# A causal attention between two mixture-of-experts layers: POOL's scatters and gathers held to the attention's steps, six scatters a step, and the causal mask added by 64-row products

## The chip, the core and the metric

The kernel runs on one core of one Trainium2 chip. TensorE (PE) multiplies matrices into PSUM, ScalarE (ACT) and VectorE (DVE) work on tiles in SBUF and PSUM, GpSimd (POOL) does some elementwise work and issues the indirect DMAs, SyncE (SP) issues most plain DMAs. Each engine runs its own list of instructions in order and waits at semaphores for the others. The metric is the device time in microseconds of one execution, as the median of several runs.

## The reference

Three blocks follow one another on x of 16 x 256 tokens and 128 features (4096 tokens in all), each on a layer norm of x:

```python
x = x + 0.5 * ffn(layernorm(x))          # first FFN
x = x + attention(layernorm(x))
x = x + 0.5 * ffn(layernorm(x))          # second FFN

# attention: 16 heads of 64, causal
logits = (x @ P_q) @ (x @ P_k).T / 8
logits = where(causal, logits, -inf)
y = sum over heads of softmax(logits) @ (x @ P_v) @ P_o.T

# ffn: 64 experts of width 64, 8 per token
scores = sigmoid(x @ gate_w.T)
# of 8 groups of experts the best 4, in these the best 8 experts (with gate_bias)
tw = 2.5 * scores[chosen] / sum(scores[chosen])
y = sum over chosen e of tw[e] * (silu(x @ Wg[e]) * (x @ Wu[e])) @ Wd[e]
y = y + shared expert
```

## The kernel before

**The FFNs.** The tokens are eight chunks of 512. Each FFN computes four chunks densely and four sparsely. Dense: all experts for every token, two experts a slot, 33 slots a chunk: the product with We_gate (L824), with We_up (L828), silu (L868), the gated product (L890), the weight of the expert (L903), the product with We_down (L840). Sparse: each token's normalised row is written once for each of its 8 experts into the DRAM array x_rows, sorted by expert, by indirect DMAs of POOL (`dispatch`, L488; 128 scatters of 128 rows for the 16 tiles of 128 tokens). SP then loads x_rows in quads of 512 rows (`f2q_xq`, L742), TensorE turns them (L582), multiplies with the expert of each tile (L607), turns the hidden values (L616) and multiplies with We_down in 64-row products (L636); SP stores the result into y_rows. 52 quads make one FFN: four of the shared expert, which need no load, and 48 with one. POOL fetches the eight results of each token back with indirect DMAs (`gather`, L524), and VectorE adds them with their weights (L542).

**The order of the second FFN.** Dense chunk 0 (33 slots and 5 to drain), then all quads, then the other three dense chunks, in which the gathers are added. The load of the first quad waits until all 128 scatters have landed (`r.scattered`), as does POOL's `copy_high` (L727), which comes after the scatters on POOL and copies We_down rows for the quads. On SP the first load stands behind the store of the first dense chunk (L2102).

**The attention.** It runs in 64 steps: 16 rows (batches) of 256 tokens, four heads a step. Step k on TensorE: the products for q, k and v of step k (L1193 to L1213; v waits for `oT_done`, VectorE's copy of the step before last), the output product of step k-2 (L1281), four transposes of the probabilities of step k-1 (L1249), the scores of the first pair of heads (`score`, L1228, then the mask L1232), eight transposes (L1249), at one step in four the transposes of the next row and of y, the scores of the second pair, in 26 of the steps a product for the second FFN's routing in the bank of k (`in_k_bank`: L1140, L1148, the count, the ranks L209 and L210, the mix), and the weighing of the values of step k-1 (`weigh_values`, L1264). A score product contracts over 64 channels and uses half of the array's rows, head 0 the lower half, head 1 the upper. The mask is added by a further product into the same bank: an identity of 128 rows (`ident_b`) times a mask of 0 and -1e30 (`mask`), both bf16, 256 columns for one head.

ScalarE in step k: the exponentials of step k-1 (`exp_done` after each pair), the copies of q and k (`k_read`), three copies of the transposed probabilities (`probT_done`, L1386), the copy of v (`v_read`, L1369). VectorE: the copy of oT (L1496), `normalise` of both pairs (L1482, L1487), the additions of gathered rows, the layer norm statistics, the maxima of the first pair (L1504, L1505, then L1508), routing of the second FFN, the maxima of the second pair.

**POOL in the attention.** Its list is written step by step: three gathers of the first FFN's results (up to step 42), the reciprocal root of a layer norm where one is due (L1018 and L1021, L1557 and L1562), and from step 49 (`A_DISPATCH`) one half tile of scatters, 4. Nothing in the list waits for the step itself: POOL runs ahead until it meets a buffer that is in use, a layer norm that VectorE has not prepared, or an index list that is not placed (`idx_done`). The remaining scatters stand at the start of the second FFN. There each is followed by a memset of a spare tile (L143, `space`).

Of the kernel before, what the change touches and what calls it, by code (L numbers as in the profile page):

```python
# [25 lines left out]
H = 16  # L26
# [122 lines left out]
def router(ctx, nc, tag, order, w, x_all, b, x_rows, f):  # L149
# [27 lines left out]
    def on_tensor(pe, misc, take_misc):  # L177
# [21 lines left out]
        def count():  # L199
            last = max(r.n for r in order if r.sparse >= 0)  # L200
            pe.wait_ge(route_step, steps_before(order, last + 1))
            pe.wait_ge(w["padded"], 1)
# [36 lines left out]
    def on_vector(dve, misc):  # L239
# [139 lines left out]
        def plan(i):  # L379
# [12 lines left out]
            elif i == 2:  # L392
                dve.wait_ge(w["padded"], 1)
# [77 lines left out]
    def on_gpsimd(pool):  # L471
# [10 lines left out]
        def dispatch(i, spaced=True):  # L482
            tile, half = divmod(i, 2)
            k, t = divmod(tile, CT)
            if t == 0 and half == 0:
                pool.wait_ge(idx_done, k + 1)
            for j in HALVES[half]:
                nc.gpsimd.indirect_dma_start(  # L488
                    x_rows[:, :], bass.IndirectOffsetOnAxis(ap=b.idx[:, f, CT * k + t, j:j + 1], axis=0),
                    b.xk[:, k, t, :], None).then_inc(scattered, 16)  # L490
                if spaced:
                    b.space(pool)
# [542 lines left out]
GATHER_STEP, ADD_LAG = 3, 4  # L1035


def attention(nc, w, x_all, banks, psum, rows, b, mix_rows, y_rows, first, second, gathered, added):
# [16 lines left out]
    with ExitStack() as ctx:  # L1055
# [61 lines left out]
        def lists_of(k):  # L1117
            return range(max(GATHER_STEP * k, 0), min(max(GATHER_STEP * (k + 1), 0), SPARSE * CT * TOPK))
# [9 lines left out]
        def _(pe):  # L1128
# [87 lines left out]
            def score(c, k, pair):  # L1216
# [333 lines left out]
        def _(pool):  # L1550
# [72 lines left out]
def ffn_first(nc, w, x_all, psum, b, mix_rows, x_rows, y_rows, zero, r, rows, x, dr):  # L1623
# [6 lines left out]
    with ExitStack() as ctx:  # L1630
# [189 lines left out]
        def _(pool):  # L1820
# [21 lines left out]
            nc.gpsimd.memset(w["mask"][:, :], 0.0).then_inc(const_step, 1)  # L1842
            nc.gpsimd.memset(w["ident_b"][:, :], 0.0).then_inc(const_step, 1)
            pool.wait_ge(const_step, 9)
            nc.gpsimd.affine_select(out=w["before"][:, :], in_=w["before"][:, :], compare_op=ALU.is_gt, fill=0.0,
                                    base=0, pattern=[[1, P]], channel_multiplier=-1)
            nc.gpsimd.tensor_copy(w["tile_no"][:, :], w["tile_i"][:, :])
            mask = w["mask"][:, :].rearrange("p (a b) -> p a b", a=2)
            nc.gpsimd.affine_select(out=mask, in_=mask, compare_op=ALU.is_ge, fill=MASKED, base=0,
                                    pattern=[[0, 2], [-1, P]], channel_multiplier=1)  # L1850
            nc.gpsimd.affine_select(out=w["ident_b"][:, :], in_=w["ident_b"][:, :], compare_op=ALU.not_equal,
                                    fill=1.0, base=0, pattern=[[-1, P]], channel_multiplier=1)\
                .then_inc(w["padded"], 1)

            waiting = list(FIRST[1:])
            for i, slot_ in enumerate(SCATTER_AT):
# [4 lines left out]
                dispatch(i)  # L1861
# [79 lines left out]
def ffn_second(nc, w, x_all, psum, b, mix_rows, x_rows, y_rows, r, out, dispatched, gathered, added):  # L1941
# [5 lines left out]
    with ExitStack() as ctx:  # L1947
# [127 lines left out]
        def _(pool):  # L2075
            rstd_of, dispatch = r.on_gpsimd(pool)
            gather = comb.on_gpsimd(pool)
            for i in range(dispatched, 2 * SPARSE * CT):
                if i == dispatched + 3:
                    rstd_of(in_dense[0])  # L2080
                dispatch(i)
# [42 lines left out]
def macaron(nc, x, P_q, P_k, P_v, P_o, gate_w, gate_bias, We_gate, We_up, We_down, Ws_gate, Ws_up, Ws_down, out):  # L2124
# [10 lines left out]
    with ExitStack() as ctx:  # L2135
# [6 lines left out]
        w["ident_b"], w["mask"] = sb("ident_b", [P, P], BF16), sb("mask", [P, 2 * P], BF16)  # L2142
# [22 lines left out]
        ffn_second(nc, w, x_all, psum, b, mix_rows, x_rows, y_rows, second, out_v, tiles // (SEQ // P) * (H // 4) - A_DISPATCH,  # L2165
# [24 lines left out]
```

## Time and profile before

| | us |
|---|---|
| median of 3 runs | 1611.32 (1610.64 to 1612.96) |
| the profiled execution | 1613.64 |
| its span in the profile | 1611.9 |
| TensorE busy | 1528.5 (95%) |
| VectorE busy | 1166.3 (72%) |
| ScalarE busy | 766.3 (48%) |
| POOL busy | 722.5 (45%) |

The stages follow one another: the first FFN up to about 540 us, the attention to about 1109 us, then the second FFN, with its first dense chunk up to 1203 us, the quads up to about 1342 us, and three dense chunks. The granted clock of TensorE, averaged over the span, is 0.984 of 2.4 GHz. How to read it: a busy share says little here, since the engine that is waited for differs from stage to stage. What a stage costs is read from the chain of waits and from the idle time that stands in brackets before an instruction.

### The profile page before, as it was taken

To read this page: it belongs to the slowest core of one execution; us is meant where nothing else is said; L and a number is where in the kernel's file an instruction comes from. 1 tells how busy PE (TensorE), PEld (TensorE's weight loads), DVE (VectorE), ACT (ScalarE), POOL (GpSimd) and SP (SyncE) were. 2 spreads that over 40 slices of the span, in tenths; PEclk is the share of its full clock that TensorE was granted. 3 is DMA by queue.
4 is the path that set the end of the run, shared out by engine and by line. 5 is a ranking of instruction groups with operands and counts; after the bars stand their busy time and mean duration, and the time that the engine had idled before them with its cause. 6 is when DMAs were issued, how large, how long until landed. Compare 5 with 4: busy or idle time off the path is not lost. (4 is left out here: it accounts for less than half of the span.)

```text
span 1611.9 us, 27350 instructions
## 1 busy us (share of the span) xinstructions
PE 1528.5 (95%) x8683; PEld 971.2 (60%) x8683; DVE 1166.3 (72%) x3354; ACT 766.3 (48%) x2105; POOL 722.5 (45%) x1123
## 2 busy tenths in 40 slices
PE   5899999999999899999999998999997999999998
PEld 2344444444788677777777776775446885444443
DVE  4698888765444588989898988765875845768675
ACT  2234223222455577777777776774224552222222
POOL 1000088888222344333334105443883225878730
PEclk9999999999999899999999999999998999999999
DMA  9999655553687111000000001103464884666652
GB/s 184 206 259 249 156 127 140 131 142 93 176 223 206 48 28 28 21 21 21 26 21 24 11 2 38 37 31 92 125 157 135 228 224 112 147 149 146 136 132 65
DMA packets 202043, 181.31 MB, mean 112 GB/s; under 512 B 39408, under 2 KB 154288, under 8 KB 201904
## 3 DMA queue, kind: packets, MB, share of 16 engines
q1 hardware_dynamic: 175056, 132.34, 34.8%
q0 software_dynamic: 16384, 33.59, 7.7%
q10 hardware_dynamic: 10464, 13.63, 2.5%
q8 instruction: 74, 1.21, 0.3%
q14 instruction: 65, 0.53, 0.1%
HBM read 121.83 MB, written 57.67 MB: 111 GB/s over the span
## 5 line engine op out<-in xcount | busy, mean ns | idle before, releaser
L868 ACT ACTIVATE f_hid<-banks 128x512 f32<-128x512 f32 (+1 forms) x264 | 157.6, 597 | 511.6 <-PE banks L828 511.5
L488 POOL DMA_INDIRECT x_rows<-r_xk,r_idx x256 | 264.4, 1033 | 138.6 <-issue 53.3
L890 DVE TENSOR_TENSOR f_hid<-banks,f_hid 128x512 f32<-128x512 f32 (+1 forms) x264 | 181.5, 687 | 145.1 <-ACT f_hid L868 144.9
L840 PE MATMUL banks<-f_hid,wd 128*128 128x512 f32 x528 | 273.3, 601 | 12.5 <-DVE f_hid L903 12.5
L824 PE MATMUL banks<-r_xT_d,gu 128*128 128x512 f32 x528 | 276.4, 605 | 4.7 <-DMA wd<-in_L_ffn_We_down 3.1
L828 PE MATMUL banks<-r_xT_d,gu 128*128 128x512 f32 x528 | 273.5, 600 | 0.0
L903 DVE TENSOR_TENSOR f_hid<-f_mix_wide,f_hid 128x512 f32<-128x512 f32 x256 | 176.0, 687 | 31.9 <-DMA f_mix_wide<-mix_rows 29.5
L840 PEld LDWEIGHTS banks<-f_hid,wd 128*128 128x128 f32 x528 | 99.6, 192 | 146.3 <-issue 120.9
L828 PEld LDWEIGHTS banks<-r_xT_d,gu 128*128 128x128 f32 x528 | 100.8, 191 | 130.1 <-issue 126.5
L824 PEld LDWEIGHTS banks<-r_xT_d,gu 128*128 128x128 f32 x528 | 97.5, 192 | 120.3 <-issue 110.6
L524 POOL DMA_INDIRECT a_g<-y_rows,r_idx x128 | 125.1, 977 | 66.3 <-issue 35.2
L1386 ACT COPY a_probT<-banks 128x512 f32<-128x512 f32 x192 | 106.2, 588 | 101.9 <-PE banks L1249 101.0
L524 POOL DMA_INDIRECT f_g<-y_rows,r_idx x128 | 128.9, 1007 | 41.2 <-issue 20.2
L1487 DVE TENSOR_SCALAR a_prob<-a_prob,a_inv 128x128 f32<-128x128 f32 (+1 forms) x512 | 130.8, 323 | 4.5
L1351 ACT ACTIVATE a_prob<-banks,a_bias 128x256 f32<-128x256 f32 x256 | 127.7, 499 | 0.0
L1228 PE MATMUL banks<-a_kT,a_qT 64*128 64x128 f32 (+1 forms) x1024 | 119.3, 351 | 0.0
L1348 ACT ACTIVATE a_prob<-banks,a_bias 128x128 f32<-128x128 f32 x256 | 99.6, 389 | 30.6 <-DVE a_bias L1508 30.5
L1249 PE MATMUL banks<-ident,a_prob 128*128 128x128 f32 x768 | 106.1, 275 | 2.5 <-ACT a_qT L1361 2.1
L143 POOL MEMSET r_spare<- 128x256 f32 x324 | 106.6, 329 | 0.2
L1264 PE MATMUL banks<-a_probT,a_v 128*64 128x256 f32 (+1 forms) x1024 | 97.3, 332 | 1.5 <-ACT a_probT L1386 0.3
L1249 PEld LDWEIGHTS banks<-ident,a_prob 128*128 128x128 f32 x768 | 89.4, 142 | 12.4 <-issue 3.5
L1504 DVE TENSOR_REDUCE a_top<-banks 128x2 f32<-128x256 f32 x128 | 53.4, 417 | 59.2 <-PE banks L1232 58.4
(243 smaller groups left out, 2879.5 us busy)
## 6 DMA issues: line engine op xcount, KB each, us to landing
f_mix_wide<-mix_rows SPq DMA_DIRECT2D x124, 512.0 KB
x_rows<-zero ACTq DMA_DIRECT2D x12, 1024.0 KB, 5.9
f1q_xq<-x_rows SPq DMA_DIRECT2D x48, 256.0 KB, 3.2
y_rows<-f1q_yq SPq DMA_DIRECT2D x48, 256.0 KB, 2.5
f2q_xq<-x_rows SPq DMA_DIRECT2D x48, 256.0 KB, 3.4
y_rows<-f2q_yq SPq DMA_DIRECT2D x48, 256.0 KB, 2.8
x_rows<-r_xk,r_idx POOLq DMA_INDIRECT x256
wd<-in_L_ffn_We_down SPq DMA_DIRECT2D x7, 512.0 KB, 10.8
```

The costliest lines, as they stand in the source:

```text
L488: nc.gpsimd.indirect_dma_start(x_rows[:, :], bass.IndirectOffsetOnAxis(ap=b.idx[:, f, CT * k + t, j:j + 1], axis=0), b.xk[:, k, t, :], Non ...
L524: nc.gpsimd.indirect_dma_start(g_buf[:, t % GBUFS, j, :], None, y_rows[:, :], bass.IndirectOffsetOnAxis(ap=b.idx[:, f, t, j:j + 1], axis=0 ...
L824: nc.tensor.matmul(gate_bank[g % 3][0:rows, :], w["gu"][:, 0, experts, :].rearrange("p e f -> p (e f)"), x, start=True, stop=True)
L828: nc.tensor.matmul(up_bank[g % 3][0:rows, :], w["gu"][:, 1, experts, :].rearrange("p e f -> p (e f)"), x, start=True, stop=True).then_inc( ...
L840: mm = nc.tensor.matmul(acc[:, :], w["wd"][0:rows, 2 * p, :], d.hid[0:rows, g % HIDS, :], start=(p == 0), stop=(p == PAIRS))
L868: nc.scalar.activation(d.hid[0:rows, g % HIDS, :], gate_bank[g % 3][0:rows, :], ACT.Silu)\
L890: nc.vector.tensor_tensor(d.hid[0:rows, g % HIDS, :], up_bank[g % 3][0:rows, :], d.hid[0:rows, g % HIDS, :], ALU.mult).then_inc(gated, 1)
L903: nc.vector.tensor_tensor(d.hid[:, g % HIDS, :], d.mix_wide[:, n % 2, p % SPREAD, :], d.hid[:, g % HIDS, :], ALU.mult).then_inc(weighted, 1)
L1228: nc.tensor.matmul(scores[pair][h][:, cols], qT[side_rows, i, pair, rows_q], kT[side_rows, i, pair, cols_k], start=(cols.start == 0), stop ...
L1249: mm = nc.tensor.transpose(bank[:, j * P:(j + 1) * P], prob[:, n * P:(n + 1) * P], w["ident"][:, :])
L1351: e = nc.scalar.activation(prob[:, o + P:o + NPB], scores[pair][h][:, P:NPB], ACT.Exp, bias=bias[:, i, pair, 1, h:h + 1], scale=HD ** -0.5 ...
L1487: m = nc.vector.tensor_scalar(prob[:, a:b], prob[:, a:b], inv[:, i, pair, late, h:h + 1], None, ALU.mult)
```

## The change

Three things change.

1. **Scatters.** From step 49 on six scatters are issued in a step of the attention (`SCATTER_STEP`) instead of four. `dispatch` takes a range of single scatters now instead of the number of a half tile. The second FFN starts with those that are left.
2. **POOL's gates.** In each step k POOL's three parts, one gather or two scatters each, wait for a point of that step (`reach`): part 0 for the exponentials of the first pair of step k-1, part 1 for the copy of k, part 2 for the last copy of the transposed probabilities.
3. **The mask.** Identity and mask are stored twice as wide, so that each half of the array's rows holds, in two parts, the 128 rows that it needs: part 0 for query rows 0 to 63, part 1 for 64 to 127. A mask of one head is now two products of 64 rows. For two heads there are four, in the order head 0, head 1 of part 0, head 0, head 1 of part 1. The products have 256 columns as before. POOL builds the two tiles in eight selects on 64 partitions each instead of two on 128, one after another.

```diff
-        def dispatch(i, spaced=True):
-            tile, half = divmod(i, 2)
-            k, t = divmod(tile, CT)
-            if t == 0 and half == 0:
-                pool.wait_ge(idx_done, k + 1)
-            for j in HALVES[half]:
+        def dispatch(lists, spaced=True):
+            for i in lists:
+                tile, j = divmod(i, TOPK)
+                k, t = divmod(tile, CT)
+                if t == 0 and j == 0:
+                    pool.wait_ge(idx_done, k + 1)
                 nc.gpsimd.indirect_dma_start(
                     x_rows[:, :], bass.IndirectOffsetOnAxis(ap=b.idx[:, f, CT * k + t, j:j + 1], axis=0),
                     b.xk[:, k, t, :], None).then_inc(scattered, 16)
...
-GATHER_STEP, ADD_LAG = 3, 4
+GATHER_STEP, SCATTER_STEP, ADD_LAG = 3, 6, 4
...
-                for h in range(2):
-                    diagonal = scores[pair][h][:, :].rearrange("p (a n) -> p a n", a=2)[:, :, 0:P]
-                    mm = nc.tensor.matmul(diagonal, w["ident_b"][:, :], w["mask"][:, :], start=False, stop=True)
+                for part in range(2):
+                    for h in range(2):
+                        side_rows = slice(h * HD, (h + 1) * HD)
+                        diagonal = scores[pair][h][:, :].rearrange("p (a n) -> p a n", a=2)[:, :, 0:P]
+                        mm = nc.tensor.matmul(diagonal, w["ident_b"][side_rows, part, :], w["mask"][side_rows, part, :],
+                                              start=False, stop=(part == 1))
                 mm.then_inc(scores_done, 1)
...
+            def reach(k, part):
+                if k < 1:
+                    return
+                if part == 0:
+                    pool.wait_ge(exp_done, 2 * k - 1)
+                elif part == 1:
+                    pool.wait_ge(k_read, k + 1)
+                else:
+                    pool.wait_ge(probT_done, 3 * k)
+
             for k in range(STEPS):
-                for i in lists_of(k):
-                    gather(i // TOPK, (i % TOPK,), spaced=False)
-                if k >= A_DISPATCH:
-                    dispatch(k - A_DISPATCH, spaced=False)
+                fetched = lists_of(k)
+                for part in range(GATHER_STEP):
+                    reach(k, part)
+                    for i in fetched[part:part + 1]:
+                        gather(i // TOPK, (i % TOPK,), spaced=False)
+                    if k >= A_DISPATCH:
+                        m = SCATTER_STEP * (k - A_DISPATCH) + 2 * part
+                        dispatch(range(m, m + 2), spaced=False)
...
+            for side in range(2):
+                for part in range(2):
+                    mask = w["mask"][side * HD:(side + 1) * HD, part, :].rearrange("p (a b) -> p a b", a=2)
+                    nc.gpsimd.affine_select(out=mask, in_=mask, compare_op=ALU.is_ge, fill=MASKED, base=part * HD,
+                                            pattern=[[0, 2], [-1, P]], channel_multiplier=1).then_inc(const_step, 1)
...
-            for i in range(dispatched, 2 * SPARSE * CT):
-                if i == dispatched + 3:
-                    rstd_of(in_dense[0])
-                dispatch(i)
+            dispatch(range(dispatched, dispatched + 12))
+            rstd_of(in_dense[0])
+            dispatch(range(dispatched + 12, TOPK * SPARSE * CT))
```

On TensorE, in a plain step of the attention, from the transposes L1249 (L1252 after the change) to the weighing of the values. Before:

```order
L1249 MATMUL banks<-ident,a_prob 128x128 x4
L1228 MATMUL banks<-a_kT,a_qT 128x128 x2
L1228 MATMUL banks<-a_kT,a_qT 128x256 x2
L1232 MATMUL banks<-mask,ident_b 128x2x128 x2
L1249 MATMUL banks<-ident,a_prob 128x128 x8
L1228 MATMUL banks<-a_kT,a_qT 128x128 x2
L1228 MATMUL banks<-a_kT,a_qT 128x256 x2
L1232 MATMUL banks<-mask,ident_b 128x2x128 x2
L1264 MATMUL banks<-a_probT,a_v 64x256 x2
```

After:

```order
L1252 MATMUL banks<-ident,a_prob 128x128 x4
L1228 MATMUL banks<-a_kT,a_qT 128x128 x2
L1228 MATMUL banks<-a_kT,a_qT 128x256 x2
L1234 MATMUL banks<-mask,ident_b 128x2x128 x4
L1252 MATMUL banks<-ident,a_prob 128x128 x8
L1228 MATMUL banks<-a_kT,a_qT 128x128 x2
L1228 MATMUL banks<-a_kT,a_qT 128x256 x2
L1234 MATMUL banks<-mask,ident_b 128x2x128 x4
L1267 MATMUL banks<-a_probT,a_v 64x256 x2
```

The mask has four products where it had two, all in the form of the score products; what stands before and behind them is the same.

On POOL, the last gathers and the start of the scatters in the attention, up to the second FFN (L1018 is a layer norm's rstd, L488 the scatter, L1055 and L2074 the ends of blocks). Before:

```order
L1018 TENSOR_TENSOR n_veps<-n_moments,eps 128x2
L1021 TENSOR_TENSOR n_rstd<-n_veps,minus_half 128x2
L488 DMA x_rows<-r_xk,r_idx 24576x128 x12
L1018 TENSOR_TENSOR n_veps<-n_moments,eps 128x2
L1021 TENSOR_TENSOR n_rstd<-n_veps,minus_half 128x2
L488 DMA x_rows<-r_xk,r_idx 24576x128 x16
L1018 TENSOR_TENSOR n_veps<-n_moments,eps 128x2
L1021 TENSOR_TENSOR n_rstd<-n_veps,minus_half 128x2
L488 DMA x_rows<-r_xk,r_idx 24576x128 x32
L1055 UNCONDITIONAL_BRANCH
L2074 UNCONDITIONAL_BRANCH
```

After:

```order
L1018 TENSOR_TENSOR n_veps<-n_moments,eps 128x2
L1021 TENSOR_TENSOR n_rstd<-n_veps,minus_half 128x2
L488 DMA x_rows<-r_xk,r_idx 24576x128 x18
L1018 TENSOR_TENSOR n_veps<-n_moments,eps 128x2
L1021 TENSOR_TENSOR n_rstd<-n_veps,minus_half 128x2
L488 DMA x_rows<-r_xk,r_idx 24576x128 x24
L1018 TENSOR_TENSOR n_veps<-n_moments,eps 128x2
L1021 TENSOR_TENSOR n_rstd<-n_veps,minus_half 128x2
L488 DMA x_rows<-r_xk,r_idx 24576x128 x48
L1055 UNCONDITIONAL_BRANCH
```

The scatters of the attention grow from 60 to 90 at the same places among the others, and the pairs of L488 and L143 that open the second FFN fall from 68 to 38. On the same engine a step's three gathers, with their waits after the change:

```order
L524 DMA a_g<-y_rows,r_idx 128x128 [waits a_exp_done]
L524 DMA a_g<-y_rows,r_idx 128x128 [waits a_k_read]
L524 DMA a_g<-y_rows,r_idx 128x128 [waits a_probT_done]
L1560 TENSOR_TENSOR r_veps<-r_moments,eps 128x2 [waits a_c_ln]
L1565 TENSOR_TENSOR r_rstd<-r_veps,minus_half 128x2 [waits a_c_rstd]
```

The gathers stood there as one row, nine for three steps; the order against the layer norms is unchanged, only the waits are new.

## Rows read from the trace of the kernel before

**Rows 1.** The page: the chain that ended last, shares of the span by line.

```profile
PE banks L824 5%; PE banks L828 5%; PE banks L840 5%; POOL x_rows L488 4%; PE banks L607 3%; PE banks L636 2%; PE banks L582 2%; POOL r_spare L143 1%; PE banks L616 1%; DVE f_hid L890 0%; DVE f_hid L903 0%; DVE x_all L542 0%; DMA f2q_xq<-x_rows 0%; DMA x_rows<-r_xk,r_idx 0%; DVE x_all L909 0%
```

**Rows 2.** The chain in order of time: start us, us, what.

```profile
1213.70 2.28 DMA x_rows<-r_xk,r_idx
1215.99 2.92 DMA f2q_xq<-x_rows
```

**Rows 3.** TensorE's timeline, quads of the second FFN: start us, us, what, [idle before].

```profile
1218.95 1.11 PE L582 MATMUL banks<-ident,f2q_xq 128*128 128x128 f32 x4 [9.44 <-DMA f2q_xq<-x_rows]
...
1226.18 0.66 PE L582 MATMUL banks<-ident,f2q_xq 128*128 128x128 f32 x4
1226.67 1.06 PE L607 MATMUL banks<-gu,f2q_xqT 128*128 x8
...
1229.02 1.06 PE L607 MATMUL banks<-gu,f2q_xqT 128*128 x8
```

**Rows 4.** Windows: busy us of PE, PEld, DVE, ACT, POOL; granted clock, DMA share, GB/s.

```profile
545.00:1105.00 560.00, 541.11 (x4524) 420.03 (x4524) 468.57 (x1665) 418.43 (x1437) 195.85 (x227) 1.00 0.08 23
...
1219.00:1224.00 5.00, 5.00 (x26) 4.45 (x27) 1.02 (x3) 1.34 (x3) 0.53 (x2) 0.50 0.38 108
```

**Rows 5.** Waits over the whole span: us in total, times, longest us.

```profile
DVE a_top L1504 <- PE banks L1232: 58.4, 55, 4.4
...
PE banks L1211 <- DVE a_oT L1496: 16.1, 13, 2.2
```

**Rows 6.** Timelines of POOL and of SP in the second FFN.

```profile
1110.66 0.96 POOL L488 DMA_INDIRECT x_rows<-r_xk,r_idx  x1 [41.13 <-POOLq L1055]
...
1112.11 0.96 POOL L488 DMA_INDIRECT x_rows<-r_xk,r_idx  x1 [0.17 <-issue]
...
1204.26 0.37 SPq L2102 DMA_DIRECT2D out<-x_all  x1
```

**Rows 7.** TensorE's timeline, one attention step, and the last score products alone.

```profile
1058.11 0.38 PE L1193 MATMUL banks<-n_xT_hi,pq_hi 128*128 128x256 f32 x1
...
1061.20 0.60 PE L1249 MATMUL banks<-ident,a_prob 128*128 128x128 f32 x4
1061.73 0.93 PE L1228 MATMUL banks<-a_kT,a_qT 64*128 64x128 f32 x8
1062.59 0.39 PE L1232 MATMUL banks<-mask,ident_b 128*128 128x256 bf16 x2
1062.81 1.04 PE L1249 MATMUL banks<-ident,a_prob 128*128 128x128 f32 x8
1063.78 0.93 PE L1228 MATMUL banks<-a_kT,a_qT 64*128 64x128 f32 x8
...
1065.07 1.52 PE L1264 MATMUL banks<-a_probT,a_v 128*64 128x256 f32 x16
1066.52 0.39 PE L1193 MATMUL banks<-n_xT_hi,pq_hi 128*128 128x256 f32 x1
...
1062.05 0.60 PE L1228 MATMUL banks<-a_kT,a_qT 64*128 64x256 f32 x4
...
1062.28 0.38 PE L1228 MATMUL banks<-a_kT,a_qT 64*128 64x256 f32 x1
```

**Rows 8.** ScalarE's timeline in that step.

```profile
1064.41 0.60 ACT L1369 COPY a_v<-banks 128x512 f32<-128x512 f32 x1
```

**Rows 9.** VectorE's and POOL's timelines in that step; L1508: ns min/median/max.

```profile
1059.10 1.01 DVE L1487 TENSOR_SCALAR a_prob<-a_prob,a_inv 128x128 f32<-128x128 f32 x4
...
1064.07 0.37 DVE L1508 TENSOR_SCALAR a_bias<-a_top 128x4 f32<-128x4 f32 x1
...
1063.51 0.95 POOL L488 DMA_INDIRECT x_rows<-r_xk,r_idx  x1 [0.30 <-issue]
1064.77 0.96 POOL L488 DMA_INDIRECT x_rows<-r_xk,r_idx  x1 [0.30 <-issue]
...
L1508 DVE TENSOR_SCALAR a_bias<-a_top x126: 169/170/405, 546.2 to 1099.9; 128x4 f32<-128x4 f32 x126
```

More of the change, by code:

```diff
@@ L201, in count @@
             pe.wait_ge(route_step, steps_before(order, last + 1))
-            pe.wait_ge(w["padded"], 1)
+            pe.wait_ge(w["padded"], 4)
             take_misc(count_read, 1)
@@ L392, in plan @@
             elif i == 2:
-                dve.wait_ge(w["padded"], 1)
+                dve.wait_ge(w["padded"], 4)
                 ins = V.tensor_copy(scan[:, 0, PAD:], b.cnt_p[:, :])
@@ L1841, in _ @@
             nc.gpsimd.iota(w["tile_i"][:, :], [[P, CT]], base=0, channel_multiplier=CHUNK).then_inc(const_step, 1)
-            nc.gpsimd.memset(w["mask"][:, :], 0.0).then_inc(const_step, 1)
-            nc.gpsimd.memset(w["ident_b"][:, :], 0.0).then_inc(const_step, 1)
+            nc.gpsimd.memset(w["mask"][:, :, :], 0.0).then_inc(const_step, 1)
+            nc.gpsimd.memset(w["ident_b"][:, :, :], 0.0).then_inc(const_step, 1)
             pool.wait_ge(const_step, 9)
             nc.gpsimd.affine_select(out=w["before"][:, :], in_=w["before"][:, :], compare_op=ALU.is_gt, fill=0.0,
-                                    base=0, pattern=[[1, P]], channel_multiplier=-1)
@@ L1847, in _ @@
[L1847 to L1853, printed above, removed]
+                                    base=0, pattern=[[1, P]], channel_multiplier=-1).then_inc(const_step, 1)
@@ new lines, in _ @@
+            nc.gpsimd.tensor_copy(w["tile_no"][:, :], w["tile_i"][:, :]).then_inc(const_step, 1)
+            pool.wait_ge(const_step, 11)
+            done = 11
+            for side in range(2):
[3 more added lines that the diff above has]
+                                            pattern=[[0, 2], [-1, P]], channel_multiplier=1).then_inc(const_step, 1)
+                    pool.wait_ge(const_step, done + 1)
+                    ident = w["ident_b"][side * HD:(side + 1) * HD, part, :]
+                    nc.gpsimd.affine_select(out=ident, in_=ident, compare_op=ALU.not_equal, fill=1.0, base=part * HD,
+                                            pattern=[[-1, P]], channel_multiplier=1)\
+                        .then_inc(w["padded"], 1)
+                    done += 1
+                    pool.wait_ge(w["padded"], 2 * side + part + 1)
@@ L1860, in _ @@
                     pool.wait_ge(zeroed, 16 * len(CLEAR_AT))
-                dispatch(i)
+                dispatch(range(4 * i, 4 * i + 4))
             copy_high = qd.on_gpsimd(pool)
@@ L2077, in _ @@
             gather = comb.on_gpsimd(pool)
-            for i in range(dispatched, 2 * SPARSE * CT):
-                if i == dispatched + 3:
-                    rstd_of(in_dense[0])
-                dispatch(i)
+            dispatch(range(dispatched, dispatched + 12))
+            rstd_of(in_dense[0])
+            dispatch(range(dispatched + 12, TOPK * SPARSE * CT))
             copy_high = qd.on_gpsimd(pool)
@@ L2141, in macaron @@
         w["gw"], w["bias"], w["ident"] = sb("gw", [P, E]), sb("gate_bias", [P, E]), sb("ident", [P, P])
-        w["ident_b"], w["mask"] = sb("ident_b", [P, P], BF16), sb("mask", [P, 2 * P], BF16)
+        w["ident_b"], w["mask"] = sb("ident_b", [P, 2, P], BF16), sb("mask", [P, 2, 2 * P], BF16)
         w["ones"], w["before"] = sb("ones", [P, P], BF16), sb("before", [P, P], BF16)
@@ L2164, in macaron @@
             attention(nc, w, x_all, banks, psum, rows, b, mix_rows, y_rows, first, second, gathered, added)
-        ffn_second(nc, w, x_all, psum, b, mix_rows, x_rows, y_rows, second, out_v, tiles // (SEQ // P) * (H // 4) - A_DISPATCH,
+        ffn_second(nc, w, x_all, psum, b, mix_rows, x_rows, y_rows, second, out_v, SCATTER_STEP * (tiles // (SEQ // P) * (H // 4) - A_DISPATCH),
                    gathered, added)
```

## The prediction

> **What bounds the kernel now.** I read the page first: its busy table and its chain of waits. TensorE is busy for 95% of the span and its lines head the chain, but the chain also holds two of POOL, L488 and L143, with 4% and 1% [rows 1]. L488 is the scatter of token rows into x_rows, L143 the memset that spaces scatters in the second FFN. So there is one place where POOL sets the time.
>
> The chain in order of time finds it [rows 2]: scatters, of which the last is issued at 1213.70 us, 2.28 us until the last one has landed, 2.92 us for the first load of gathered rows (f2q_xq), then TensorE's transposes of L582. TensorE's timeline shows what that costs [rows 3]: L582 starts at 1218.95 after 9.44 us idle, released by that load. The windows show the granted clock: 0.50, so 1.2 GHz, from 1219 to 1224 [rows 4]; in the attention it is 1.00 (2.4 GHz). A quad step is 2.35 us long afterwards (L607 at 1226.67 and at 1229.02), but the first two behind the wait take 7.23 us together (L582 at 1218.95 and, as third, at 1226.18) [rows 3]. The wait therefore costs 9.44 + 7.23 - 4.70 = 12.0 us.
>
> Elsewhere the end is set by TensorE itself. In the attention it is busy 541.11 of 560 us [rows 4], and a plain step is 8.40 us long (first L1193 at 1058.11 and at 1066.52) [rows 7]. The exceptions are 13 steps in which its L1211 (project_v) waits for VectorE's copy of oT, 16.1 us in total and 2.2 at most [rows 5]. There VectorE is behind with the routing of the second FFN. So an instruction more or less on TensorE counts in about 51 of 64 steps.
>
> **Scatter, six a step.** Steps 49 to 63 are 15; at 4 each they issue 60 scatters, at 6 each 90. Left for the second FFN are 38 instead of 68. There a scatter takes 1.46 us with its spacer (1110.66 to 1112.11) [rows 6], so POOL ends 30 x 1.46 = 43.8 us earlier, at about 1170. In the attention one takes 1.26 us (1063.51 to 1064.77) [rows 9]. Six take 7.6 us of an 8.4 us step, and with the row's rstd, in two of the steps, 8.5: POOL just keeps up, and those rstd have two steps until they are used.
>
> What is late once the scatters are not? SP issues the loads behind the store of x_all at 1204.26 [rows 6]. The load then lands at about 1204.26 + 0.37 + 2.92 = 1207.6, up to 1 us later behind the store's own 256 KB. TensorE wants it at 1218.95 - 9.44 = 1209.5. That is hidden, and TensorE has no idle time that would take its clock down. copy_high of POOL starts 44 us earlier too. I take the full -12.0; a load 1 us late would make it about -11.
>
> **The mask by 64-row products.** Before, TensorE goes from 64-row score products to two products on all 128 rows (L1232), then to transposes (L1249). After, four 64-row products stand in two concurrent pairs. Two of L1228's products start together here: four of its entries start between 1062.05 and 1062.28, in two passes 0.22 us apart [rows 7]. A mask product streams 256 columns in bf16, 0.11 us, so two pairs cost 0.22, as the two products do now (1062.59 to 1062.81). The multiplication is not what changes. What changes is where the array changes between forms.
>
> The prices, from starts in [rows 7]. Eight transposes take 0.97 us until L1228 starts, four take 0.53: 0.11 each and 0.09 for going to the 64-row form. The last score pass starts at 1062.28 and the mask at 1062.59, 0.31 instead of 0.22: 0.09 for going back. In the quads L636 is a 64-row product in front of transposes: leaving it costs the same 0.09, and then four transposes L582 take 0.49 (1226.18 to 1226.67) instead of 0.44 [rows 3], another 0.05 while the first weights load uncovered. Behind the bf16 mask that second part is 0.01. So for pair 0 the change moves the switch from a place where it costs 0.10 to one where it costs 0.15: +0.05 us a step. Pair 1 is followed in 26 steps by a product in the k bank (another +0.05 in most), else by weigh_values (L1264). There one switch goes entirely, 0.10. But in a plain step L1264 does not start for that reason: it starts at 1065.07, 0.05 us after a_v is copied (1064.41 + 0.60), and on ScalarE that copy stands behind the two copies of probT which the eight transposes release [rows 7, 8]. The saved 0.10 becomes waiting, and the +0.05 of pair 0 passes through. Only some 5 steps, with a_v early, gain it.
>
> The sum: 51 x 0.05 = 2.6, k bank 22 x 0.05 = 1.1, less 5 x 0.10 = 0.5. scores_done comes up to 0.10 earlier, which shortens the 13 places where VectorE sets the time by 0.05 to 0.10, so less 1.0. Together +2.2 us. Bounds: -2 if entering the transposes costs no more than entering the mask did, +5 if every step pays twice.
>
> The Trainium skill, TensorEngine Tiling (Array Packing), Key Properties, says that changing the tiling mode, not just the tile, drains TensorE. The rows agree that a change costs (0.09 us). Counted by that rule alone a step has five changes instead of six and nothing gets slower, which is my first rival below; the row of L582 says that the changes are not equal in price.
>
> **POOL held to the steps.** Gathers now go out one at each of three points of ScalarE's step instead of nine in a row. They are added four steps later and land in a few us, so VectorE never waits for one; a gather's wait for `added` was met 1 to 2 steps earlier. POOL's rstd come behind the last gather of their step and are used two steps on. What can change is a clash on VectorE. L1508 takes 0.17 us, but 0.37 when it starts at 1064.07, and it ends at 1064.44, with POOL's scatter (1063.51 + 0.95) [rows 9]. Most are not hit: of 126 the median is 170 ns. The first point, exp_done of pair 0, is what releases VectorE's four tensor_scalar of normalise as well, so a hit there becomes regular. In a plain step it is hidden, since the first group of L1487, pair 0's, is done at 1060.11 and the first transposes start at 1061.20 [rows 7, 9]. Where VectorE is behind (13 places, each with some two steps of backlog) up to 0.1 us a step is added, and hits in the old runs of nine go away. I take +0.5, between -1.5 and +3.
>
> The Trainium skill, SBUF — State Buffer, Who interferes with whom, says that a tensor_scalar in a two-port mode and a GpSimd instruction exclude each other completely. The L1508 row agrees, with 0.20 us for one hit; by that rule alone every held issue could hit, and this speaks against the change.
>
> **The rest.** At the start POOL builds mask and ident_b in eight selects with waits instead of two. It ends these at about 10 us and their first use is hundreds of us later: 0. Four more products' instructions on TensorE are hidden in the pairs.
>
> Sum: -12.0 + 2.2 + 0.5 = -9.3 us. The profiled execution took 1613.6 us with a span of 1611.9; the median of the runs is 1611.3. Against it: **1602.0 us**.
>
> **The rivals.**
> 1. The switches are worth the same everywhere, so the attention gains a little: pair 0 -0.01 x 51, five steps -0.10, VectorE's places -1.0, so -2.0, and no clash. -14.0: 1597.3. For it: one change of form less. Against it: L582 behind L636. Chance 0.20.
> 2. The clashes become regular: 13 places x 2 steps x 0.1 x 1 to 2 hits, about +4 instead of +0.5: 1605.5. For it: the shared release. Against it: VectorE is idle 55 times before L1504, 58.4 us in total [rows 5], which absorbs most. Chance 0.13.
> 3. A load or copy_high takes the scatter's place at 1209 and TensorE still idles 2 to 3 us with half the clock behind: gain of 6 to 8 us less 2.7, 1606. Against it: SP has only one store ahead. Chance 0.06.
> 4. The slower side: the 64-row mask products do not run as pairs but one after another, as they write into two banks with a strided pattern that L1228 does not have. Each mask then costs 2 x 0.11 more, 128 x 0.22 = 28 us. Of the 13 waits on VectorE, eight stand alone, one in every four steps, with some 1.1 us each, and absorb 9; the five late ones, 0.4 each, 2. 28 - 11 - 12.0 + 0.5 = +5.5: 1617. It decides from the point where more than half of the second products start 0.1 us after the first. Against it: L1228's pairs start 0.01 apart. Chance 0.06.
> The forecast itself: 0.55.
>
> **How the numbers follow.** Forecast's own range: 1599.5 to 1604.5. With the rivals 1 to 3 the range is 1597 to 1607.5, outside it rival 4 and the tails. About 0.2% (3.2 us) is what a measurement here can tell from no change. Faster: forecast, rivals 1 and 2 and nearly all of 3, 0.90; same 0.04; slower, rival 4 in most of its cases, 0.06.
>
> **What would show it.** Right: L582's wait for f2q_xq is gone, granted clock 1.00 at 1209 to 1215, POOL's last L488 some 44 us earlier; the mask products' starts in pairs 0.01 apart; L1228 to mask 0.22, mask to L1249 0.20, and four or eight transposes 0.05 longer; plain steps 8.45 us instead of 8.40. Wrong: plain steps of 8.40 or less (rival 1), the L1211 waits over 17 us in total (rival 2), L582 still waiting (rival 3), mask products 0.11 apart four times (rival 4).

## The result, and the profile after

The changed kernel takes 1601.53 us (median of 6 runs, 1599.03 to 1604.78), the kernel before 1611.34 beside it; the ratio is 0.9933, with a 95% interval of 0.9913 to 0.9952. Forecast were 1602.0, between 1597.0 and 1607.5. An execution now and then takes several per cent longer at a lower granted clock; one such of e6 (1744.52 us) is left out of its median below.

The span is 1601.1 us instead of 1611.9. Milestones of TensorE's timeline divide both. (The first eight quads make seven entries of L582 in the timeline, since the first entry holds two.)

| stretch | before | after | after - before | forecast |
|---|---|---|---|---|
| attention, first L1193 to the dense run's L824 | 578.60 | 580.66 | +2.06 | +2.7 |
| dense run, to the first quad | 93.28 | 94.80 | +1.52 | 0 |
| start of the first quad to start of the eighth | 25.19 | 13.14 | -12.05 | -12.0 |
| ahead of the attention | 531.46 | 530.31 | -1.15 | 0 |
| all from the eighth quad on | 383.39 | 382.15 | -1.24 | 0 |

**The wait is gone.** TensorE's timeline after, columns as in [rows 3]:

```profile
1205.77 1.04 PE L582 MATMUL banks<-ident,r_xk 128*128 128x128 f32 x8
...
1211.23 0.72 PE L636 MATMUL banks<-wd,f2q_hidT 64*128 64x128 f32 x8
1211.87 0.66 PE L582 MATMUL banks<-ident,f2q_xq 128*128 128x128 f32 x4
...
1214.22 0.66 PE L582 MATMUL banks<-ident,f2q_xq 128*128 128x128 f32 x4
...
1216.56 0.66 PE L582 MATMUL banks<-ident,f2q_xq 128*128 128x128 f32 x4
```

The first L582 on f2q_xq has no bracket: no idle time, where [rows 3] shows 9.44 us. The quads follow at 2.35 us from the first on. The window, and then POOL's timeline, say why:

```profile
1211.00:1216.00 5.00, 5.00 (x49) 4.25 (x47) 3.56 (x9) 2.66 (x7) 0.00 (x0) 1.00 0.29 82
```

```profile
1170.75 1.05 POOL L488 DMA_INDIRECT x_rows<-r_xk,r_idx  x1 [0.17 <-issue]
1171.80 0.33 POOL L143 MEMSET r_spare<- 128x256 f32 x1
1178.35 0.52 POOL L727 COPY f2q_wd_high<-wd 128x128 f32 x2 [6.23 <-DMA x_rows<-r_xk,r_idx]
```

The granted clock is 1.00 where [rows 4] has 0.50, and the last scatter is issued 43 us earlier than in [rows 2]. In the chain's shares POOL no longer stands:

```profile
PE 27%; DVE 3%; ACT 0%; issue 0%
```

**The attention step.** TensorE's timeline, a plain step of after:

```profile
1059.17 0.39 PE L1193 MATMUL banks<-n_xT_hi,pq_hi 128*128 128x256 f32 x1
...
1060.66 0.28 PE L1211 MATMUL banks<-pv_hi,n_xT_hi 128*128 128x256 f32 x1
...
1061.34 1.02 PE L1284 MATMUL banks<-a_oT,po 128*128 128x256 f32 x4
1062.20 0.60 PE L1252 MATMUL banks<-ident,a_prob 128*128 128x128 f32 x4
1062.73 0.93 PE L1228 MATMUL banks<-a_kT,a_qT 64*128 64x128 f32 x8
1063.49 0.39 PE L1234 MATMUL banks<-mask,ident_b 64*128 64x256 bf16 x4
1063.81 1.09 PE L1252 MATMUL banks<-ident,a_prob 128*128 128x128 f32 x8
1064.83 0.93 PE L1228 MATMUL banks<-a_kT,a_qT 64*128 64x128 f32 x8
```

Against [rows 7]: scores to mask 0.76 instead of 0.86, mask to transposes 0.32 instead of 0.22, eight transposes 1.02 instead of 0.97. The sum from L1228 to L1228 is 2.10 instead of 2.05, the +0.05 of the prediction. But the step is still 8.40 long, for its projections are quicker. Here L1193 to L1211 takes 1.49 us and L1211 to L1284 0.68. The same step before, whose [rows 7] are continued here:

```profile
1059.63 0.28 PE L1211 MATMUL banks<-pv_hi,n_xT_hi 128*128 128x256 f32 x1
...
1060.33 1.03 PE L1281 MATMUL banks<-a_oT,po 128*128 128x256 f32 x4
```

takes 1.52 and 0.70: its projections start 0.118 us apart, while after they start 0.114 apart. Of 23 plain steps 19 have the slow spacing before and none after. Steps with a product in the k bank have no such gift (8.46 to 8.55 us, 9.07 to 9.21). The waits on VectorE's copy of oT, after, over the whole span:

```profile
DVE a_top L1507 <- PE banks L1234: 55.5, 54, 4.3
...
PE banks L1211 <- DVE a_oT L1499: 16.1, 13, 2.1
```

Their total of 16.1 us is that of [rows 5].

### The profile page after: what moved, and what is told of

Its sections match the earlier page's. It is cut to its first block and busy times, and to the rows that moved or that the text cites. A ratio compares the mean times of both kernels' runs of the same rounds, so it can differ in the third digit from the quotient of the medians.

```text
span 1601.1 us, 27870 instructions
## 1 busy us (share of the span) xinstructions
PE 1523.2 (95%) x8939; PEld 974.9 (61%) x8939; DVE 1167.1 (73%) x3354; ACT 766.1 (48%) x2105; POOL 717.4 (45%) x1099
## 5 line engine op out<-in xcount | busy, mean ns | idle before, releaser
L488 POOL DMA_INDIRECT x_rows<-r_xk,r_idx x256 | 263.3, 1028 | 125.8 <-issue 51.6
L824 PE MATMUL banks<-r_xT_d,gu 128*128 128x512 f32 x528 | 275.4, 603 | 4.2 <-DMA wd<-in_L_ffn_We_down 2.6
L824 PEld LDWEIGHTS banks<-r_xT_d,gu 128*128 128x128 f32 x528 | 97.3, 192 | 119.5 <-issue 109.9
L1389 ACT COPY a_probT<-banks 128x512 f32<-128x512 f32 x192 | 106.2, 588 | 104.4 <-PE banks L1252 103.5
L1228 PE MATMUL banks<-a_kT,a_qT 64*128 64x128 f32 (+1 forms) x1024 | 119.9, 353 | 0.0
L1252 PE MATMUL banks<-ident,a_prob 128*128 128x128 f32 x768 | 109.7, 279 | 2.5 <-ACT a_qT L1364 2.1
L1252 PEld LDWEIGHTS banks<-ident,a_prob 128*128 128x128 f32 x768 | 86.8, 142 | 24.7 <-issue 16.3
L143 POOL MEMSET r_spare<- 128x256 f32 x294 | 96.7, 329 | 0.2
L1507 DVE TENSOR_REDUCE a_top<-banks 128x2 f32<-128x256 f32 x128 | 53.3, 417 | 55.6 <-PE banks L1234 55.5
```

The costliest lines, as they stand in the source:

```text
L488: nc.gpsimd.indirect_dma_start(x_rows[:, :], bass.IndirectOffsetOnAxis(ap=b.idx[:, f, CT * k + t, j:j + 1], axis=0), b.xk[:, k, t, :], Non ...
L824: nc.tensor.matmul(gate_bank[g % 3][0:rows, :], w["gu"][:, 0, experts, :].rearrange("p e f -> p (e f)"), x, start=True, stop=True)
L1228: nc.tensor.matmul(scores[pair][h][:, cols], qT[side_rows, i, pair, rows_q], kT[side_rows, i, pair, cols_k], start=(cols.start == 0), stop ...
L1252: mm = nc.tensor.transpose(bank[:, j * P:(j + 1) * P], prob[:, n * P:(n + 1) * P], w["ident"][:, :])
```

## The experiments

They ran on four chips, and these fall into two kinds. On two the kernel before takes 1613 to 1614 us (e9 to e11 on one, e12 on another). On the other two it takes 1761 (e1 to e4, and e5 to e8), which nothing in the first two profiles had announced. Each chip ran one batch only, so whether this belongs to the chip or to something else at that hour isn't shown; I speak of chips. So each ratio is to the kernel before on its own chip, and stretches are compared between chips only where the steps repeat to 0.01 us.

| run | what it is | us | ratio to before, 95% | attention | first to eighth quad |
|---|---|---|---|---|---|
| e1 | before + new mask | 1764.48 | 1.0036 [1.0014, 1.0057] | 729.4 | 25.6 |
| e2 | before + gates | 1625.35 | 0.9241 [0.9213, 0.9269] | 593.2 | 27.3 |
| e3 | before + six scatters | 1790.25 | 1.0184 [1.0154, 1.0214] | 766.6 | 13.1 |
| e4 | before + six + gates | 1622.92 | 0.9224 [0.9196, 0.9251] | 603.0 | 13.1 |
| e5 | after | 1630.62 | 0.9257 [0.9230, 0.9285] | 612.4 | 13.1 |
| e6 | before, 1 memset between | 1690.92 | 0.9608 [0.9571, 0.9645] | 655.6 | 27.3 |
| e7 | after, one gate | 1663.44 | 0.9455 [0.9424, 0.9486] | 638.4 | 13.1 |
| e8 | after, mask by head | 1628.04 | 0.9246 [0.9220, 0.9272] | 608.8 | 13.1 |
| e9 | before + five + gates | 1601.22 | 0.9939 [0.9919, 0.9959] | 578.7 | 13.1 |
| e10 | before, 3 memsets between | 1615.24 | 1.0021 [1.0009, 1.0034] | 580.6 | 25.4 |
| e11 | after, 1 memset behind each | 1609.17 | 0.9976 [0.9963, 0.9988] | 587.1 | 13.1 |
| e12 | after, no gates | 1599.52 | 0.9924 [0.9907, 0.9941] | 578.9 | 13.1 |

### e1 to e4: one part at a time

```
e1:  + the four 64-row mask products, mask and ident_b in halves
e2:  + reach(k, part)                     (SCATTER_STEP = 4, old mask)
e3:  + SCATTER_STEP = 6                   (no reach, old mask)
e4:  + SCATTER_STEP = 6, + reach(k, part) (old mask)
```

> The kernel before with the 64-row mask products alone; four scatters a step, POOL not held. Theory (the mask moves a switch of the array's form in front of the transposes): steps with a product in the k bank 0.09 to 0.14 us longer, steps with project_v waiting for VectorE unchanged or shorter, attention +1 to +2 us in the trace, the wait of 9.4 us for f2q_xq stays: 1611 to 1613 us, ratio 1.000 to 1.001. Rival (the longer attention is POOL's doing, the mask is free): attention as before within 0.3 us. Rival (fewer switches pay): attention 1 to 2 us shorter.

> The kernel before with POOL held to the steps alone; four scatters a step, mask by 128-row products. Theory (holding makes hits on VectorE's tensor_scalar regular): VectorE's tensor_scalar grow by about 3 us in total over the attention, the 13 waits of project_v by up to 0.05 us each, attention +0 to +1 us, time 1611 to 1613. Rival (holding spreads the gathers and relieves VectorE): attention up to 1 us shorter, 1610.

> The kernel before with six scatters a step alone; POOL not held, mask by 128-row products. Theory: the whole gain comes from here: the wait for f2q_xq and the clock that falls behind it go, -12.0 us against before, attention within 0.3 us: 1599 to 1600 us, 1.5 to 3 us faster than the changed kernel. Rival (without the gates 30 more scatters crowd the last 15 steps and lengthen them by 0.1 us each or more): 1601 or more.

> Six scatters a step and POOL held, mask by 128-row products: the changed kernel without its mask. Theory (three parts that add up): e3 plus what e2 adds, attention 0 to 1 us longer than before, 1599 to 1601 us. Rival (gates matter only with six scatters, by spreading them): shorter than e3 by 0.5 us or more.

All four times were missed, since the forecasts knew only the first kind of chip. The parts can still be read. The last column settles the scatters: six a step take 25.6 or 27.3 us to 13.1, gates or no gates, mask old or new. TensorE's L582 of e2, which keeps four scatters, shows the old wait (11.57 us), and e4's shows none:

```profile
1234.91 1.11 PE L582 MATMUL banks<-ident,f2q_xq 128*128 128x128 f32 x4 [11.57 <-DMA f2q_xq<-x_rows]
```

```profile
1233.53 0.66 PE L582 MATMUL banks<-ident,f2q_xq 128*128 128x128 f32 x4
```

The attention refutes what all theories said of the gates: without them it is 150 to 190 us longer than in the first profile, with them 15 to 24. What stands still is seen in ScalarE's, POOL's and TensorE's timelines of e1:

```profile
789.46 0.58 ACT L1364 COPY a_qT<-banks 128x512 f32<-128x512 f32 x1 [0.40 <-PE banks L1213]
795.17 0.58 ACT L1380 COPY a_kT<-banks 128x512 f32<-128x512 f32 x1 [5.12 <-remote]
```

```profile
787.63 0.95 POOL L524 DMA_INDIRECT a_g<-y_rows,r_idx  x1 [0.30 <-issue]
788.88 1.07 POOL L524 DMA_INDIRECT a_g<-y_rows,r_idx  x1 [0.30 <-issue]
790.26 0.94 POOL L524 DMA_INDIRECT a_g<-y_rows,r_idx  x1 [0.30 <-issue]
...
794.11 0.94 POOL L524 DMA_INDIRECT a_g<-y_rows,r_idx  x1 [0.30 <-issue]
```

```profile
795.85 0.59 PE L1228 MATMUL banks<-a_kT,a_qT 64*128 64x128 f32 x2 [5.03 <-issue]
```

The kernel before was timed on these chips but not profiled; e1 is its nearest relative. L1380 waits for scores two steps back, the value that L1364 had already been let through on, and for the k projection, whose last product (L1195) started at 788.21. Everything it needs is there, yet it starts 5.12 us late, just after POOL's eighth indirect DMA in a row. TensorE's scores wait for it. In the first profile POOL issues the same row of eight at the same speed (739.27 to 749.35), and ScalarE isn't held up:

```profile
743.17 0.60 ACT L1361 COPY a_qT<-banks 128x512 f32<-128x512 f32 x1
743.63 0.62 ACT L1377 COPY a_kT<-banks 128x512 f32<-128x512 f32 x1
```

I counted such late wakes: waits of ScalarE and VectorE in the attention's own chain that end more than 0.5 us after the engine was free and the last semaphore was raised, by how many indirect DMAs POOL had issued back to back when the wait could have ended:

```
             0 or 1      2        3        4      5 and more
before       0/598     0/18     0/33     0/34      0/197
e1           4/646     8/16     1/17     8/18     22/43
e2           0/797     0/48     7/14    16/16       -
e4           1/784     6/65     3/10     9/19       -
e5           4/788     3/52     4/8     13/21       -
```

The other five traces of quiet chips (after, e9 to e12) have none either. So on these chips late wakes belong to runs of indirect DMAs, and the gates keep the runs short.

The longest stand in POOL's last and longest run, 32 scatters back to back in e1 (1141.37 to 1181.65). ScalarE's and VectorE's timelines:

```profile
1186.71 1.07 ACT L1389 COPY a_probT<-banks 128x512 f32<-128x512 f32 x2 [23.21 <-remote]
```

```profile
1186.84 0.42 DVE L1507 TENSOR_REDUCE a_top<-banks 128x2 f32<-128x256 f32 x1 [33.78 <-remote]
```

The transposes for L1389 were done at 1155.00 and its engine was free at 1163.50, so it is 23 us late; the mask products for L1507 were done at 1165.68, so it is 21 us late. Both go on within 0.13 us of each other, 5 us after POOL's last issue has ended. This one step (56) takes 47.4 us, and 68.7 in e3, where the run has 48 scatters and the maxima are 47 us late; in the first profile, with the same run of 32, it takes 8.36. Steps 50, 52 and 56 are also where e3, with its longer runs, loses against e1: 10.6, 10.7 and 21.3 us of some 37. The windows of the attention, before and e1, divide the 151 us of e1:

```profile
532.00:1110.00 578.00, 554.99 (x4613) 430.57 (x4611) 475.53 (x1688) 426.93 (x1461) 205.99 (x238) 0.99 0.08 23
```

```profile
532.00:1261.00 729.00, 593.26 (x4869) 459.76 (x4869) 477.17 (x1690) 430.05 (x1461) 205.75 (x238) 0.91 0.07 18
```

TensorE is idle for 136 us instead of 23, and what is left comes with the granted clock, 0.91 instead of 0.99.

### e5 to e8: run, density, or running ahead

```
e6:  gather(..., spaced=True), dispatch(..., spaced=True)    (before, in the attention)
e7:  reach: part 0 waits for exp_done; parts 1 and 2 no wait (after)
e8:  for h in range(2): for part in range(2):                (after, loops swapped)
```

> The changed kernel itself, unaltered, beside the next three. On the chip of the first four runs ScalarE's and VectorE's waits of the attention ended 0.5 to 12.7 us after the semaphore was raised when POOL had issued two or more indirect DMAs back to back (16 of 16 waits behind the fourth of a run with gates and four scatters), and never behind a first one (0 of 269). If that chip comes again: theory (late wakes belong to runs, the gates cut them) about 1625, two us over the 1622.7 of gates and six scatters with the old mask; rival (the new mask lets VectorE start earlier into POOL's issues) 1618. If a chip without late wakes comes: 1602.

> The kernel before, with one memset of the spare tile (0.33 us) between any two indirect DMAs of the attention and nothing else changed; no gates. Theory A (late wakes come from back-to-back issue): with a pause of some 0.6 us between two of them the attention falls from about 730-750 us to under 620 and the time from 1761 to 1640 or less. Theory B (they come from POOL running several steps ahead, however it is spaced): no change, 1740 to 1770. On a chip without late wakes both say 1611, and DVE may lose up to 3 us to the memsets.

> The changed kernel with one gate a step instead of three: POOL waits for the first pair's exponentials and then issues the step's three gathers, and from step 49 six scatters too, back to back. Theory A (length of the run): second and third of a run are late in about half of the waits, the runs of six to nine from step 49 in most: 1660 to 1720 us on the chip with late wakes. Theory B (holding POOL to the step is enough): 1620 to 1630, as with three gates. On a chip without late wakes: 1602 plus or minus 3, which is then the price of clashes alone.

> The changed kernel with the mask's four products of a pair in the order head 0 part 0, head 0 part 1, head 1 part 0, head 1 part 1 instead of part by part; nothing else. Theory A (neighbours on different halves of the array pass together, neighbours on the same half one after the other): three passes of 0.11 us a pair instead of two, 0.22 us a step more, +14 us over the changed kernel on the same chip. Theory B (only the written pairs go together, four passes): +0.44 a step, +28 us. Theory C (the order makes no difference, the two halves keep their own queues): +0 to 2 us.

e5: the changed kernel there takes 1630.62, above both values that I had put down; the comparison with e4 crosses two chips, so the 8 us between them aren't a price of the mask. In steps 12 to 47 (the first is step 0), where neither has late wakes, they differ by 322.75 - 320.50 = 2.25 us, and that is the mask.

e6: 1691, between the theories. Spacing by one memset takes about half of the extra away (the attention is 77 us over the quiet 578.6, where e1, on the other such chip, is 151 over), and late wakes remain even behind a first or second DMA (13 of 175). Its waits in the attention:

```profile
DVE a_top L1504 <- remote: 48.9, 18, 8.3
ACT a_probT L1386 <- remote: 18.8, 15, 3.8
```

e7: 1663, 97 us less than the kernel before, where three gates give 130. That lies in theory A's range, and the late wakes go with the length of the run: 0 of 169 behind a second DMA, 21 of 79 behind a third, 18 of 19 behind a fifth or sixth. Theory A had foretold more behind a second. The run can't part holding from length, though: one gate holds POOL to the step, and it also cuts the runs from up to 32 DMAs to three and, from step 49, six. Theory B, that holding alone is enough, is refuted.

e8: 1628.04 against 1630.62 of e5, with intervals that overlap: theory C. Nearly every undisturbed step is as long as e5's to 0.01 us (steps 12 to 47: 322.61 and 322.75). The order in which the products of the two halves are written costs nothing.

### e9 to e12: chips without late wakes

```
e9:   SCATTER_STEP = 5 (2, 2, 1 behind the gates), old mask
e10:  three memsets between two indirect DMAs of the attention (before)
e11:  one memset behind each indirect DMA of the attention (after)
e12:  - reach(k, part)                                          (after)
```

> The changed kernel with five scatters a step (two, two, one behind the three gates) instead of six, and the mask's products as they were before; the rest as changed. Theory A (the dense run hides what is left: POOL's last scatter, 44 us earlier with six, is some 20 us earlier with five, and the wait was 9.4): L582's wait at the fifth quad is gone as with six, and on the chip with late wakes the attention lies between 593 (four) and 603 (six) us: 1618. Theory B (five aren't enough, part of the wait stays): 1622 to 1628. On a chip without late wakes: 1599 (A), 1603 to 1608 (B).

> The kernel before with three memsets of the spare tile (1 us) between any two indirect DMAs of the attention instead of none (one memset gave 1692 against 1761); no gates. Theory A (what counts is how densely the indirect DMAs follow each other): attention under 620 us, late wakes nearly gone, 1640 to 1655 in spite of scatters that end later. Theory B (a share of the trouble is POOL running ahead of the step, however spaced, or POOL being busy at all): no better than with one memset, 1680 to 1700. On a chip without late wakes: 1611 to 1622, by the scatters that slip.

> The changed kernel with one memset (0.33 us) behind each indirect DMA of the attention. Theory A (density): the last fifteen steps, 9.6 to 13.6 us each on the chip with late wakes, fall towards 8.5, and the time from 1631 to 1610 to 1618. Theory B (POOL is then busy for nearly all of such a step, and its memsets meet VectorE): no gain, 1628 to 1640. On a chip without late wakes: 1601 to 1604.

> The changed kernel without its three gates a step: three gathers, and from step 49 six scatters, back to back from the step's start; everything else as changed. On a chip without late wakes, theory A (the gates are worth nothing there: five scatters with gates gave the attention the same 578.6 us as before): 1600 to 1604, the wait at the fifth quad gone by the six scatters alone. Theory B (without gates the denser issue costs VectorE's operations what the gates save): 1605 to 1610. On a chip with late wakes (1761 before), both: 1770 to 1800, as six scatters without gates gave 1790.

e9: theory A by the wait, 2 us over its time. POOL's last scatter is issued at 1191.41, and the L582 that had waited has no bracket:

```profile
1191.41 1.14 POOL L488 DMA_INDIRECT x_rows<-r_xk,r_idx  x1 [0.17 <-issue]
```

```profile
1208.01 0.66 PE L582 MATMUL banks<-ident,f2q_xq 128*128 128x128 f32 x4
```

22 us of advance cure a wait of 9.4 as well as 43 do. The attention has the same 578.65 us as before: gates and a fifth scatter are free here.

e10: what it was sent for can't be seen, since its chip had no late wakes. It takes 1615.24, inside the range given for such a chip: the attention is 2.0 us longer, 1.2 of it at its end (see e11), and the scatters that slip make the wait longer:

```profile
1223.53 1.12 PE L582 MATMUL banks<-ident,f2q_xq 128*128 128x128 f32 x4 [10.86 <-DMA f2q_xq<-x_rows]
```

e11: both theories missed, 1609 instead of 1601 to 1604. Six scatters with a memset each want 6 x 1.46 = 8.8 us of an 8.4 us step, so POOL falls behind, and TensorE waits for it at the stage's end:

```profile
1121.11 2.05 PE L824 MATMUL banks<-r_xT_d,gu 128*128 128x512 f32 x2 [5.40 <-PEq L1055]
```

POOL's last instruction there ends at 1111.79, which is 3.9 us before TensorE's last (1115.70). What is waited for is POOL's DRAIN, which closes the block of the attention on each engine (L1055). Duration in ns and start, in e11 and then in the changed kernel:

```profile
L1055 POOLq DRAIN  x1: 10154/10154/10154, 1110.4 to 1110.4; - x1
```

```profile
L1055 POOLq DRAIN  x1: 10792/10792/10792, 1099.6 to 1099.6; - x1
```

It ends at 1120.5 in e11, 8.7 us behind POOL's last instruction. In the changed kernel it ends at 1110.39, also 8.7 us behind, and the last of the other engines' DRAINs at 1110.70: six scatters a step left 0.3 us there. In e10 it ends at 1113.03, and TensorE waits 2.0 us instead of 0.8.

e12: theory A, half a microsecond under its figure. Without gates 1599.52, on a quiet chip (one without late wakes) no worse than with them (0.9924 against 0.9933 and 0.9939 of e9, intervals overlap).

No variant beats the changed kernel measurably on quiet chips. On the others e4 (the old mask, 0.9224) has the best ratio, but its interval overlaps that of e5.

## Why the prediction was right

**The scatters, -12.0.** Shown, to 0.05 us: the table's third row, and e3, e4 and e12, which have six scatters with and without each other part; of the -12.05 these runs repeat the 13.14 us after. The load landed in time as worked out, and TensorE's clock stayed up.

**The mask, +2.2.** Shown: in steps 12 to 47 the old mask takes 320.4 to 320.7 us in four traces (before, e2, e4, e9), the new one 322.4 to 322.8 in four (after, e5, e8, e12), so 1.8 to 2.4 us for these 36 steps. The mechanism holds too: entering the transposes from the 64-row form costs 0.05 more than entering the mask did. Its distribution was wrong, and three terms that missed made up for each other. I put 0.05 on each of 51 steps, another 0.05 on k-bank steps, and took 1.0 off for the places where VectorE sets the time. Measured in these 36 steps (e12 against before, without gates) are -0.1 on the nine plain steps, +1.8 on 20 others, mostly 0.09 to 0.14 on each k-bank step, and +0.3 on the seven steps that end on VectorE, which got longer and not shorter.

"Plain steps 8.45 us instead of 8.40" failed as it stands: they have 2.05 to 2.10 where it was foretold, and projections 0.05 faster. By the test I had written, 8.40 spoke for rival 1, which the sum refutes. Like steps compared settle it. These are the plain steps among 2 to 47 of all 14 traces, without those that a late wake lengthens, by the spacing of their projections:

| | spacing 0.114 us | spacing 0.118 us |
|---|---|---|
| old mask | 8.33 to 8.36 us (29 steps) | 8.40 to 8.41 us (86) |
| new mask | 8.38 to 8.42 us (101) | 8.45 us (10) |

So the new mask costs the foretold 0.05 at either spacing, and what else changed is how often each spacing occurs. Why it does isn't settled. It isn't the mask alone, since both masks have steps of either kind.

Rival 4 is refuted by the step rows: four products fit into 0.32 us (0.76 + 0.32 is what 0.86 + 0.22 was), and e8 shows that they needn't be written in pairs.

**POOL held, +0.5, between -1.5 and +3.** Right for the first chip and blind for others. On quiet chips the gates are worth nothing: 578.60 without them before, 578.65 with them in e9, and 1599.52 without them in e12. Rival 2 shows its first sign only: the seven steps that end on VectorE are 9.71 and 9.99 us in e9 instead of 9.68 and 9.93, 0.3 us in all, but other steps give it back and the waits stay at 16.1 to 16.4 us. "POOL just keeps up" was closer than the prediction knew: it left out the DRAIN, and 0.3 us were left (e11). On the chips with late wakes the same gates are worth 136 us (e2), more than ten times what the wait was. Nothing in the trace of before could have told this.

**What the sum didn't have.** The dense run behind the attention took 1.5 us more. The two windows, after and then e9, show the clock:

```profile
1111.00:1136.00 25.00, 25.00 (x56) 11.06 (x57) 14.55 (x32) 7.19 (x11) 21.41 (x32) 0.94 0.73 170
```

```profile
1111.00:1136.00 25.00, 25.00 (x63) 11.32 (x62) 15.52 (x33) 7.22 (x12) 22.16 (x35) 1.00 0.75 192
```

Both are busy throughout, at 0.94 and at 1.00. Over all 14 traces this stretch takes 91.5 us (4), 93.1 to 93.5 (8) or 94.8 to 94.9 (2), with a granted clock over the whole of it of 1.00, 0.98 and 0.96. This goes with no edit: after and e5 are the same program and take 94.8 and 91.5. I put it down to chance. Step 48 of the attention, in which TensorE waits some 2 us for VectorE, does the same: it takes 12.5 to 12.6 us in nine traces, where the clock falls, and 10.9 to 11.0 in the other five (e1, e3, e8, e10, e12). Together the two can move a single profile by 5 us, half of the forecast gain. Before and after both have the long step 48, and the +1.5 of the dense run met -1.15 and -1.24 in the stretches that nothing was foretold for, which no run explains. That the sum was met to 0.5 us has some luck in it.

## What to carry to other kernels

Count a queue's slack before enlarging a fix: a wait of 9 us was gone with one scatter a step more, and the second only filled POOL, up to 0.3 us from a new wait at the end of the stage. Run a change on more than one chip before trusting a null: the gates that did nothing on quiet chips saved 8% on others. Price a switch of the array's form by what is entered behind it, and test such a price by the sum over many steps, or between steps that are alike in all else, rather than in one.

## What the runs showed of the hardware

- On two of the chips used, ScalarE and VectorE went on late while POOL issued indirect DMAs back to back: by 5 us behind a run of eight, 21 and 23 behind one of 32 (e1), 47 behind one of 48 (e3). On the others nothing was late behind the same runs of 32 and 48 (before, e12). The issue itself was no slower (median 957 ns in the attention of before, of e1 and of e2). From the fourth of a run on, half to all of the waits were late in e2 and e5. What holds them, the semaphore or the instructions behind it, these traces don't tell, nor what sets these chips apart.
- A pause of one memset isn't enough against it (e6). Behind the first DMA of a gated run 7 of 1107 waits were late (e2, e4, e5 and e8).
- The mask's four products of a pair, two on each half of the array, start two by two, 6 to 7 ns apart, also where the program writes both products of one half first (e8: 625.910, 625.916, 626.019, 626.026); the records don't name the half.
- POOL's DRAIN at the end of the attention ended 6.9 to 9.3 us after POOL's last instruction, an indirect DMA's issue or the memset behind it, in all 14 traces. It cost TensorE 4.6 us in e11 and 1.2 in e10, and nothing in the others.
- Leaving the 64-row form cost 0.10 us in front of the bf16 mask and 0.10 in front of the fp32 transposes, and these took another 0.05 (L1228 to L1228, 2.05 and 2.10 us). The first is the same at both places, only the second depends on what is entered.
